# Local transformer: the copy of a token block to its work buffer, written as the block's maximum with itself

## The reference, cut to what matters

```python
x = attn_layer(shifted(x)) + x     # qkv, per-head l2 norm, rotary, local attention in windows of 32
x = ffn_layer(shifted(x)) + x      # layer norm, W1, gelu gate, W2
```

## Time and profile before

| what | value |
|---|---|
| median of 3 runs | 2660.53 us (2656.42 to 2661.36) |
| the profiled execution's own time | 2653.32 us |
| its span in the profile | 2651.4 us |
| granted TensorE clock, mean over the span | 0.983 of full speed |
| PE busy | 2499.3 us (94%), 41090 instructions |
| PEld busy | 1924.2 us (73%) |
| DVE busy | 1974.8 us (74%), 4815 instructions |
| ACT busy | 1763.8 us (67%), 3794 instructions |
| POOL busy | 1493.6 us (56%), 1917 instructions |
| first and last start of line 2140 | 134.2 and 1829.6 us |

### The profile page before, as it was taken

How to read it: one execution, slowest core, us unless ns; L and a number is a source line. 1 busy time by engine, 2 the same in 40 slices (tenths; PEclk the granted TensorE clock), 3 DMA queues, 4 the chain that set the end, 5 groups by cost and what they waited for, 6 DMA issues and landing times.

```text
span 2651.4 us, 102895 instructions
## 1 busy us (share of the span) xinstructions
PE 2499.3 (94%) x41090; PEld 1924.2 (73%) x41090; DVE 1974.8 (74%) x4815; ACT 1763.8 (67%) x3794; POOL 1493.6 (56%) x1917
## 2 busy tenths in 40 slices
PE   7789999999999999999999999999898989999898
PEld 6657776777766777777677777777677877999667
DVE  6778887888778878888788877887466877555564
ACT  5577777777777778777777777777343357333465
POOL 5566766676666676676667667666232146000472
PEclk9999999999999999999999999999899989999999
DMA  2200000101001100110010100000002000000022
GB/s 90 68 14 16 16 12 18 33 26 27 18 23 32 32 15 22 32 30 20 18 33 26 27 18 17 13 16 17 4 4 86 0 5 6 1 0 1 13 76 80
DMA packets 56280, 66.72 MB, mean 25 GB/s; under 512 B 25097, under 2 KB 30932, under 8 KB 55380
## 3 DMA queue, kind: packets, MB, share of 16 engines
q1 hardware_dynamic: 56148, 64.87, 8.9%
HBM read 38.23 MB, written 1.05 MB: 15 GB/s over the span
## 4 chain that ended last, share of the span: by engine, by line
PE 80%; DVE 6%; issue 5%; POOL 4%; ACT 3%; DVEq 1%; SPq 0%; POOLq 0%; DMA 0%; ACTq 0%
PE ps L798 13%; PE ps L903 6%; PE ps L819 6%; PE ps L812 6%; PE ps L846 5%; PE ps L883 5%; PE ps L925 5%; PE ps L860 3%; PE ps L1017 3%; PE ps L937 3%; PE ps L893 3%; PE ps L1001 3%; PE ps L1002 3%; PE ps L744 2%; ACT area L1193 2%
## 5 line engine op out<-in xcount | busy, mean ns | idle before, releaser
L1193 ACT ACTIVATE area<-ps 128x512 f32<-128x512 f32 (+4 forms) x1520 | 762.2, 532 | 400.0 <-PE ps L789 130.3
L1669 POOL TENSOR_TENSOR area<-area 128x512 f32<-128x512 f32 x384 | 482.3, 1278 | 7.9 <-DVE area L2168 7.9
L1691 POOL TENSOR_TENSOR area<-area,mx 128x512 f32<-128x512 f32 x192 | 200.2, 1043 | 489.8 <-DVE mx L2196 489.8
L798 PE MATMUL ps<-lw,area 128*128 128x512 f32 x768 | 413.0, 620 | 1.1 <-ACT area L1193 0.7
L1683 POOL TENSOR_TENSOR area<-area,rnq 128x512 f32<-128x512 f32 x384 | 393.2, 1046 | 8.2 <-ACT rnq L1349 0.7
L1317 ACT ACTIVATE area<-ps 128x512 f32<-128x512 f32 x384 | 227.3, 592 | 87.5 <-PE ps L798 87.5
L2166 DVE TENSOR_TENSOR area<-ps,table 128x512 f32<-128x512 f32 x384 | 260.7, 679 | 7.5 <-ACT area L1317 4.7
L2168 DVE TENSOR_TENSOR area<-ps,table 128x512 f32<-128x512 f32 x384 | 261.2, 680 | 0.0
L2147 DVE TENSOR_REDUCE ssq<-area 128x8 f32<-128x512 f32 x384 | 252.0, 676 | 1.7 <-ACT area L1317 0.8
L812 PE MATMUL ps<-ident,area 128*128 128x128 f32 x1536 | 218.2, 274 | 10.5 <-POOL area L1683 7.6
L812 PEld LDWEIGHTS ps<-ident,area 128*128 128x128 f32 x1536 | 180.3, 141 | 65.2 <-issue 53.2
(11 more groups left out here) (301 smaller groups left out, 5665.0 us busy)
## 6 DMA issues: line engine op xcount, KB each, us to landing
lvm<-area SPq DMA_DIRECT2D x384, 65.0 KB
lw<-in_wqkv SPq DMA_DIRECT2D x36, 256.0 KB
area<-in_moe_w SPq DMA_DIRECT2D x24, 256.0 KB, 2.7
lw<-in_wout SPq DMA_DIRECT2D x12, 256.0 KB
ctxT<-in_ctxT SPq DMA_DIRECT2D x64, 38.5 KB, 1.8
lw<-in_moe_w SPq DMA_DIRECT2D x8, 256.0 KB, 2.9
lw<-in_wff SPq DMA_DIRECT2D x6, 341.0 KB
lw<-in_moe_g SPq DMA_DIRECT2D x1, 1152.0 KB
```

The lines of the kernel that those rows point to most:

```text
L798: nc.tensor.matmul(banks[:, lb_qk[j], :], xsT[s], wqkv[w.p][:, j * 512:(j + 1) * 512], start=True, stop=True).then_inc(l_qk_ps, 1)
L1193: return nc.scalar.activation(dst, src, ACT.Identity if kw else ACT.Copy, **kw)
L1669: pool.tensor_tensor(QR[s][:, cols], QR[s][:, cols], RA[s][:, cols], ALU.add).then_inc(l_rsum, 1)
```

## The change

One instruction is written in another form. Before, the copy is a `tensor_scalar`: it reads one tensor and multiplies it by the constant 1.0. After, it is a `tensor_tensor` that reads the same block as both of its operands and takes their maximum, which is the block itself. Output, semaphores, waits and place in the order stay as they are. The instruction is executed 96 times: 16 blocks in 6 layers.

```diff
--- before.py
+++ after.py
@@ -2137,7 +2137,7 @@
 
             def tokens(s, w):
                 follow(dve, l_y1, nth(0, w.it, s) - 2)
-                V.tensor_scalar(xw[s][:, :], Y[:, w.pr * G + s, :], 1.0, None, ALU.mult).then_inc(l_y, 1)
+                V.tensor_tensor(xw[s][:, :], Y[:, w.pr * G + s, :], Y[:, w.pr * G + s, :], ALU.max).then_inc(l_y, 1)
 
             def square_sums(s, w, j):
                 if j == 1:
```

## The result

The change made the kernel 0.18% slower: ratio 1.0018, 95% interval 1.0011 to 1.0025, from 20 runs of each (medians 2662.8 and 2656.5 us). On 2656.5 us that is 4.8 us, between 2.9 and 6.6; the two medians lie 6.3 us apart, inside that interval. The forecast was 4.2 us, within 0.2%. The profiled execution of the changed kernel took 2663.6 us with a span of 2661.7 us; the one of before took 2653.3 us. Of these 10.3 us, 6.4 lie between the first copy and the last, and the rest outside, where the change does nothing.

What follows compares the result with a forecast made beforehand. PE, running nearly back to back, bounds the kernel; the copy counts only where PE waits. Terms of 2.0, 1.5, 0.5 and 0.1 us, together 4.2 us, added to the 2660.5 us median give 2664.7 us, range 2652 to 2674 us.

Steps and rivals of the forecast that it cites:

- The copy is held as before: Line 2140 beside POOL's line 1683: new copy still waits for POOL, ends 63 ns later; 4.2 us slower, 61 in 100.
- 290 ns where it stands alone: Line 2140 without a GpSimd neighbour: the two-operand copy takes 290 ns, 63 ns more than 227.
- 28 ns to spare in 44 free copies: Nearly all in second halves: PE's line 789 has 28 ns to spare, so 44 x 35 ns = 1.5 us.
- The other terms: Costs: 32 held copies, 2.0 us; 8 free ones PE waits for, 0.5 us; 5 briefly held, 0.1 us.
- GpSimd held 50 ns longer, cost nothing: POOL's line 1683 behind a free copy is held 50 ns longer; taken as nothing, at most 0.7 us.
- Let in earlier: Rival: held copy enters up to 0.14 us early while POOL finishes writing; -0.3 us, 2660 us, 11 in 100.
- Not held: Rival: new copy does not wait for POOL's line 1683; 19.4 us gained, 2641.1 us, 13 in 100.
- Register work for the second operand: Rival: an extra 40 to 75 ns register instruction between line 2218 and the copy; 2672 to 2674 us, 14 in 100.
- The races of the sixth layer: Six copies there start at most 0.02 us ahead of line 1683; losing costs about 0.8 us each, 4.8 us.

Runs made afterwards that it cites:

- experiment 1: Copy as a scalar_tensor_tensor with the constant 1.0 (block times 1.0, maximum with the block) instead of the plain copy of the kernel before: ratio 1.0031.
- experiments 1 and 3: The third: two-operand copy in loops' first halves only, or second halves only, plain copy otherwise; against the kernel before, ratios 1.0018 and 1.0009.
- experiment 2: Copy as a scalar_tensor_tensor with a column of ones in SBUF instead of the constant; against the kernel before, ratio 1.0061, 16.2 us.

## Why the prediction was right, and where not

*The copy is held as before* (the likeliest case): right. Among the rows it rested on one in which DVE held GpSimd; the reverse is now seen 32 times, and lifting the hold in four ways gave 13 to 24 us.

*290 ns where it stands alone*: 293 ns, so 66 ns more and not 63, 0.3 us over all.

*28 ns to spare in 44 free copies*: wrong, and the term that was mis-sized, 1.5 us for what measures 64 x 44 ns = 2.8 us. I compared the copy's end with the start of the matmul of line 789. The instruction that reads the copy is the weight load of the same line, and it stood 0.13 us behind the copy in every stretch. The matmul's row began up to 28 ns later behind line 911, without that being time to spare: it does not tell when its operand was wanted.

*The other terms*: 32 held copies x 64 ns = 2.0 us, 8 x 64 = 0.5 us, 5 x 60 = 0.3 us, as forecast or nearly. With 2.8 us that makes 5.6 us. PE's late line 798 adds 0.8 us, which I had not seen (1.1 us in seven first halves, less what it gave back elsewhere). That is 6.4 us, and 6.4 us is what the profiled executions show over the copies, but so close a match is luck: the measured sum also holds the three odd stretches named under the table, together -0.65 us, and without them the other 92 make 7.0 us, 0.6 us more than these terms. The runs say 4.8 us with 6.6 as upper end. So the forecast of 4.2 us was near for the right mechanism, with one term too small by 1.3 us and one of 0.8 us missing, together half of it.

*GpSimd held 50 ns longer, cost nothing*: right. Its idle time ahead of line 1700 shrank from 0.11 to 0.06 us in second halves, and PE's waits for line 1683 went from 11.9 to 11.6 us.

*Let in earlier* fell: 0.147 us behind GpSimd's end, not 0.08. *Not held* fell with it. *Register work for the second operand* fell too: one register instruction of 75 ns at the median as before, 0.42 (0.41) and 0.16 us ahead of the copy as before.

The absolute time, 2664.7 us against 2662.8, was helped by two errors that partly cancel: the median of three runs that I started from lay 4 us above the one of twenty, and the sum was 1 to 2 us too small. The races of the sixth layer likely explain only a part of why the profiled execution lay under the median. Of the six close races one, at 1314.46 us, is in the fifth layer, and in the like kernel of experiment 1 only two that were won before were lost. The granted clock goes with the scatter much more clearly: the 20 runs of the changed kernel go from 2657.1 us at 0.984 up to 2665.7 us at 0.979, and the profiled execution of before had 0.983. At 0.983 the changed kernel took 2658.9 to 2661.6 us (six runs) and the one of before, in the experiments' rounds, 2651.6 to 2654.8 us (five runs), 6.6 us apart in the mean; as these are not the same rounds, that is a hint that the change costs nearer 6 than 5 us, and no more.

## What to carry to other kernels

When a short DVE instruction takes 0.2 us at one time and 1 us at another, look at what GpSimd runs at its start. Of the other forms tried here only the reduction was let in; two tensor operands are held just as the plain copy is, and are slower besides. Better is to change who goes first, or to give the work to an engine that was never held here (ACT's 96 copies took 301 to 311 ns); and to judge slack on PE by the weight load that reads the operand, not by the matmul.

On the hold itself the Trainium skill was right. Its page "SBUF — State Buffer", section "Who interferes with whom", says that an instruction with two SBUF inputs contends with a GpSimd instruction that reads SBUF, and one with at most one input outside the two-port modes does not; the traces agree with both (32 held of 96, and none of 96).

## What the runs showed of the hardware that was not expected

A column operand costs a free `scalar_tensor_tensor` 59 ns (352 against 293) and a held one nothing. It also seems to move the moment at which the instruction takes its turn. In the traces of before, of the changed kernel and of experiments 1 and 3, every copy that began while a line 1683 ran and no more than 4 ns behind its start went free, as did those ahead of it, and every one from 5 ns behind its start was held. With the column, seven copies that began 1 to 39 ns ahead of it were held, and those 63 ns or more ahead were not. The border has moved by 43 to 68 ns, and the 59 ns fit in.

PE's weight load of line 798 comes 1.05 us behind that of line 789 in most stretches. It comes later, by up to 0.18 us, where PE had been kept waiting a little at line 789. In the changed kernel's sixth layer, with the load of 789 at 0.28 us behind the last one of line 911, and in the same stretch of before, with 0.21 to 0.22 us:

```profile
1713.98 0.30 PEld L911 LDWEIGHTS ps<-area,shift 128*128 128x128 f32 x2
...
1714.37 0.14 PEld L789 LDWEIGHTS ps<-ident,xw 128*128 128x128 f32 x1
...
1714.62 0.86 PEld L846 LDWEIGHTS ps<-area 64*32 64x32 f32 x64
...
1715.57 0.30 PEld L798 LDWEIGHTS ps<-lw,area 128*128 128x128 f32 x2
```

```profile
1707.49 0.30 PEld L911 LDWEIGHTS ps<-area,shift 128*128 128x128 f32 x2
...
1707.82 0.14 PEld L789 LDWEIGHTS ps<-ident,xw 128*128 128x128 f32 x1
...
1708.08 0.70 PEld L846 LDWEIGHTS ps<-area 64*32 64x32 f32 x64
...
1708.86 0.30 PEld L798 LDWEIGHTS ps<-lw,area 128*128 128x128 f32 x2
```

That is 1.20 and 1.04 us. Over ten traces, where the two loads of 911 and 789 are 0.10 to 0.22 us apart line 798 follows after 1.05 us with few exceptions; at 0.25 to 0.29 us it follows after 1.12 to 1.22 us in 71 of 79 places; and from 0.32 to 0.39 us it is mostly late too, by 0.05 to 0.13 us. The added time does not stand at line 798 but in line 846, whose 64 weight loads lie between the two and take 0.86 us instead of 0.70: in each of the seven places of the changed kernel there is one pause of 0.14 to 0.15 us between the 61st and the 62nd of them, where before has 5 ns. Neither a semaphore nor an instruction of PE's sequencer stands in this pause. What it is stays open, and no run was made to settle it; it took 0.8 us of this change and 4.8 us of experiment 2.
